# Expert chunks of eight slots in place of eleven, in a mixture-of-experts feed-forward kernel

## The chip, the cores and the metric

The kernel runs on one core of a Trainium2 chip. The metric is device time in microseconds (us). Engines: TensorE (PE; its weight loads are shown as PEld), VectorE (DVE), ScalarE (ACT), GpSimd (POOL) and SyncE (SP, which issues the DMAs).
## The reference, cut to what matters

A gate picks two of four experts for each of 64 samples of 64 tokens. Each expert is a two-layer network over all tokens of its samples; experts 1 and 2 leave out one third of a sample's tokens. A shared expert runs on all 4,096 tokens. A second stage, untouched here, does a gated feed-forward on every token and one of eight small experts on listed tokens.

```python
gate_scores = jax.nn.softmax(gate_logits, axis=-1)
topk_w, topk_i = jax.lax.top_k(gate_scores, K)          # K = 2, B = 64 samples
...
mask[1, L_head:L_head + L_wrist] = 0.0                  # one third of a sample
mask[2, :L_head] = 0.0
...
for e in range(E):                                      # E = 4
    h = jax.nn.gelu(context_c @ ew1[e] + eb1[e], approximate=True)   # 256 -> 1024
    y = h @ ew2[e] + eb2[e]                                          # 1024 -> 256
    out = out + w_be[:, e][:, None, None] * mask[e][None, :, None] * y
shared = jax.nn.gelu(context_c @ sw1 + sb1, approximate=True) @ sw2 + sb2
return out + shared
```

## The kernel before, in words

Weights and activations are held as pairs of float16 parts, high and low, and a product takes three matmuls (high x high, high x low, low x high). Work is cut into chunks of columns. A shared chunk has 256 columns (four samples). A sample is 66 columns wide with its borders, in three segments of SEG = 22; a *slot* is one segment of one sample for one expert. Experts 0 and 3 need three slots of a sample, 1 and 2 two (KEPT). An expert chunk has SLOTS slots of one expert, so RC = SLOTS x 22 = 242 columns, and each expert's last chunk is filled up with empty slots.

Per chunk, PE runs `hidden` (L1152): 8 blocks of the hidden layer x 3 x 2 = 48 matmuls into the four banks ps_hidden; then `output` (L1180) of the chunk before: 2 x 8 x 3 = 48 matmuls into ps_out. ACT applies gelu (L1022), DVE splits the result into high and low parts (L1325, L1327), ACT adds the bias of the output (L1113), and DVE adds each slot, times its gate weight, to the accumulator (`add_slots`, L1608). POOL copies the slots' columns together for the chunk two ahead (`stage_columns`, L1721). Slot addresses and the expert number of each chunk stand in the row tab, of SLOTS + 1 entries a chunk, which DVE makes from the gate's choice at run time. PE reads the expert number with `expert_of` (L1163) once for each half chunk, and the weights' addresses are computed from it:

```python
def w1(e, part, db, hb):
    return W[:, bass.ds(e * WE + (part * 2048 + db * 1024 + hb * P), P)]
```

Order on PE: shared chunks 0 to 13 (two more come late), the first hidden of the expert chunks, the output of shared chunk 13, then for r = 1, 2, ...: hidden(r), output(r-1). The program is written out chunk by chunk. Chunks up to NRMIN - 1 always run; the rest, up to NR, stand each in an If within the one before (`expert_loops`), with the count read once (L301) and compared at each (L283). NR is the largest count that any choice of the gate can need, NRMIN the smallest. After the last, a branch leads past the chunks not needed, to two late shared chunks, and then stage 2. Some small jobs are tied to a chunk number: index at 13, key matmuls (L1249) at 14, compare at 16 and 17, place (L1256, L1257) at 18, pack (L1263) at 20, listed at 21. Stage 2 uses L592, L604, L612, L625, L641.

Of the kernel before, what the change touches and what calls it, by code (L numbers as in the profile page):

```python
# [30 lines left out]
ALU = mybir.AluOpType  # L31
AX = mybir.AxisListType
# [12 lines left out]
SEG = NT - 2 * HEAD  # L45
BS = 3 * SEG
CB = CH // NT
SLOTS = 11
RC = SLOTS * SEG
KEPT = (3, 2, 2, 3)  # L50
KEPT0 = (0, 0, 1, 0)
NR = (2 * 3 * NB + E * (SLOTS - 1)) // SLOTS
NRMIN = -(-2 * 2 * NB // SLOTS)
NSLOT = NR * SLOTS
ROW = SLOTS + 1
NCNT = -(-3 * NB // SLOTS)
FAR = 16384
# [22 lines left out]
def program(nc, a):  # L80
    with ExitStack() as ctx:
# [80 lines left out]
        siota = xsw[0:NB, 2 * NSLOT:4 * NSLOT].bitcast(F32)  # L162
# [805 lines left out]
        def _(sp):  # L968
            for n, (dram, place, *_) in enumerate(opening):
                sp.dma_start(place, dram).then_inc(start_in[n], 16)  # L970
                if n == 1:
                    for dst, src in ((b1[:, :], a["b1"]), (b2[:, :], a["b2"])):
                        sp.dma_start(dst, src).then_inc(first_in, 16)
# [321 lines left out]
        def _(dve):  # L1295
            steps = [0]

            def link(i):

                steps[0] += 1  # L1300
                i.then_inc(dv, 1)
                dve.wait_ge(dv, steps[0])
# [180 lines left out]
            ce = yw[0:1, 0:4 * NR].rearrange("p (k r) -> p k r", k=4)  # L1483
# [5 lines left out]

            total, even = G[0:1, 27, 0:1], G[0:1, 27, 1:2]  # L1490
            link(nc.vector.tensor_tensor(total, G[0:1, 19, E - 1:E], G[0:1, 18, E - 1:E], ALU.add))
            link(nc.vector.tensor_scalar(ce[:, 0, 0:NR // 2], siota[0:1, 0:NR:2], total, None, ALU.is_lt))
            link(nc.vector.tensor_reduce(even, ce[:, 0, 0:NR // 2], AX.X, ALU.add))
            link(nc.vector.tensor_scalar(even, even, -2.0, 1.0, ALU.mult, ALU.add))
            link(nc.vector.tensor_tensor(even, even, total, ALU.add))
            link(nc.vector.tensor_scalar(total, total, -2.0, None, ALU.add))
# [287 lines left out]
```

## Time and profile before

| | us |
|---|---|
| median of 3 runs | 607.18 (607.03 to 607.24) |
| the profiled execution | 604.62 |
| its span, first to last instruction | 602.0 |
| PE busy | 567.1 (94%) |
| PE weight loads busy | 499.6 (83%) |
| DVE busy | 409.0 (68%) |
| ACT busy | 264.3 (44%) |
| POOL busy | 178.1 (30%) |
| mean granted TensorE clock | 0.979 |

Matmuls are pipelined, so a row's mean duration of one (267 ns) is a latency and not its share of the time; the distance from start to start is. "Issue" in the chain and in the waits is time in which an engine waited for nothing that the profile shows. The sequencer's own operations are not counted as busy.

### The profile page before, as it was taken

To read this page: it belongs to the slowest core of one execution; us is meant where nothing else is said; L and a number is where in the kernel's file an instruction comes from. 1 tells how busy PE (TensorE), PEld (TensorE's weight loads), DVE (VectorE), ACT (ScalarE), POOL (GpSimd) and SP (SyncE) were. 2 spreads that over 40 slices of the span, in tenths; PEclk is the share of its full clock that TensorE was granted. 3 is DMA by queue.
4 is the path that set the end of the run, shared out by engine and by line. 5 is a ranking of instruction groups with operands and counts; after the bars stand their busy time and mean duration, and the time that the engine had idled before them with its cause. 6 is when DMAs were issued, how large, how long until landed. Compare 5 with 4: busy or idle time off the path is not lost.

```text
span 602.0 us, 17044 instructions
## 1 busy us (share of the span) xinstructions
PE 567.1 (94%) x5093; PEld 499.6 (83%) x5094; DVE 409.0 (68%) x1092; ACT 264.3 (44%) x577; POOL 178.1 (30%) x529
## 2 busy tenths in 40 slices
PE   5999999999999999999999999999999979999770
PEld 4888888876899999999999999989999958667650
DVE  4969977757565868685677888756474735686560
ACT  6666667532444434344334343434343425464320
POOL 0350000000763444443424244443434002870000
PEclk9999999999999999999999999999999979999895
DMA  8812345001001232310000000000000001922130
GB/s 272 261 46 71 105 141 170 23 1 36 2 1 38 106 107 106 107 71 3 3 2 3 1 4 1 4 2 3 1 3 4 2 4 59 359 76 71 48 129 9
DMA packets 28482, 36.93 MB, mean 61 GB/s; under 512 B 4762, under 2 KB 24115, under 8 KB 28132
## 3 DMA queue, kind: packets, MB, share of 16 engines
q1 hardware_dynamic: 28292, 35.57, 18.0%
q8 instruction: 48, 0.79, 0.5%
q14 instruction: 46, 0.38, 0.2%
q0 software_dynamic: 96, 0.20, 0.1%
HBM read 27.30 MB, written 8.53 MB: 60 GB/s over the span
## 4 chain that ended last, share of the span: by engine, by line
PE 91%; DVE 3%; issue 1%; ACT 1%; DMA 1%; SPq 1%; POOL 0%; POOLq 0%; DVEq 0%
PE ps_out L1180 40%; PE ps_hidden L1152 39%; PE ps_hidden L592 3%; PE ps_hidden L641 1%; PE ps_out L612 1%; DMA W<-in_xT 1%; PE ps_turn L625 1%; PE ps_small L625 1%; PE ps_out L1223 1%; DVE X L782 1%; PE ps_out L604 1%; DVE hbuf L1327 0%; PE ps_hidden L625 0%; SPq L970 0%; DVE W L1311 0%
## 5 line engine op out<-in xcount | busy, mean ns | idle before, releaser
L1180 PE MATMUL ps_out<-hbuf,W 128*128 128x242 f16 (+2 forms) x2304 | 250.7, 269 | 0.7 <-DVE W L1311 0.6
L1180 PEld LDWEIGHTS ps_out<-hbuf,W 128*128 (+1 forms) x2304 | 223.8, 98 | 21.0 <-issue 1.3
L1721 POOL COPY xs<-X 128x88 f16 x352 | 128.4, 414 | 287.0 <-PE ps_hidden L1152 175.1
L1022 ACT ACTIVATE h<-ps_hidden,b 128x242 f32<-128x242 f32 (+1 forms) x384 | 155.8, 467 | 79.8 <-PE ps_hidden L1152 78.0
L1152 PE MATMUL ps_hidden<-xs,W 128*128 128x242 f16 x1536 | 164.2, 267 | 0.8 <-issue 0.8
L1152 PEld LDWEIGHTS ps_hidden<-xs,W 128*128 x1536 | 149.4, 98 | 10.8 <-issue 1.6
L1327 DVE TENSOR_TENSOR hbuf<-h,hbuf 128x484 f16<-128x484 f32 (+2 forms) x192 | 129.9, 676 | 7.4
L1608 DVE SCALAR_TENSOR_TENSOR acc<-ytmp,wrow,acc 128x44 f32 (+1 forms) x352 | 65.8, 259 | 92.4 <-ACT ytmp L1113 88.0
L1152 PE MATMUL ps_hidden<-X,W 128*128 128x256 f16 (+1 forms) x768 | 92.7, 283 | 10.3 <-DVE W L1311 6.1
L1325 DVE CAST hbuf<-h 128x484 f16<-128x484 f32 (+2 forms) x192 | 84.7, 441 | 22.4 <-ACT h L1022 21.2
L1152 PEld LDWEIGHTS ps_hidden<-X,W 128*128 128x128 f16 x768 | 76.6, 100 | 23.5 <-DVE W L1311 5.8
L1113 ACT ACTIVATE ytmp<-ps_out,b 128x242 f32<-128x242 f32 (+1 forms) x64 | 26.2, 460 | 133.4 <-PE ps_out L1180 133.4
L1031 ACT ACTIVATE acc<-ps_out,b 128x256 f32<-128x256 f32 x28 | 11.7, 470 | 41.0 <-PE ps_out L1180 41.0
L947 POOL COPY W<-acc 128x2 f32 x128 | 26.1, 338 | 2.8 <-issue 2.8
L1333 DVE SCALAR_TENSOR_TENSOR W<-stage,W 128x1024 f16<-128x1024 f32 x16 | 19.3, 1220 | 5.8 <-ACT W L1041 5.7
L1041 ACT ACTIVATE W<-stage 128x1024 f16<-128x1024 f32 x16 | 17.0, 1060 | 12.5 <-DMA stage<-in_ew 12.5
L592 PE MATMUL ps_hidden<-W,F 128*128 128x512 f16 x96 | 22.2, 379 | 0.0
L592 PEld LDWEIGHTS ps_hidden<-W,F 128*128 128x128 f16 x96 | 9.3, 100 | 10.0 <-DVE W L743 0.5
L953 POOL DMA_INDIRECT out_rows<-ytmp,sid x1 | 1.0, 1024 | 47.8 <-DVE ytmp L869 47.8
L940 POOL DMA_INDIRECT ytmp<-in_xR,gid x1 | 1.6, 1564 | 43.2 <-DVE f L1661 43.2
L612 PEld LDWEIGHTS ps_out<-onesm,W 128*128 128x128 f32 x64 | 8.8, 202 | 5.6 <-issue 4.7
L612 PE MATMUL ps_out<-onesm,W 128*128 128x1 f32 x64 | 8.1, 248 | 4.2 <-DVE stage L769 4.2
(291 smaller groups left out, 297.3 us busy)
## 6 DMA issues: line engine op xcount, KB each, us to landing
stage<-in_ew SPq DMA_DIRECT2D x16, 512.0 KB, 3.7
stage<-in_xR SPq DMA_DIRECT2D x8, 512.0 KB, 3.8
moved_rows<-stage SPq DMA_DIRECT2D x8, 512.0 KB, 2.6
X<-moved_rows SPq DMA_DIRECT2D x8, 512.0 KB, 9.2
out_rows<-X SPq DMA_DIRECT2D x16, 256.0 KB, 2.2
W<-in_xT SPq DMA_DIRECT2D x7, 512.0 KB, 9.2
W<-in_fw SPq DMA_DIRECT2D x1, 2304.0 KB, 12.5
W<-in_sw SPq DMA_DIRECT2D x4, 256.0 KB, 3.3
```

The source lines that it names most:

```text
L592: mm = pe.matmul(ps1[which][:, :], fw(wp, which, db), chl[:, k % CR, 2 * xp + db, :], start=(n == 0), stop=(n == 5))
L612: mm = pe.matmul(psy[1][:, k * MG + n:k * MG + n + 1], sq[:, k % 2, n * P:(n + 1) * P], onesm[:, 0:1], start=True, stop=True)
L947: i = nc.gpsimd.tensor_copy(cgT[:, :, at + j:at + j + 1], column(cols[j]))
L1022: i = nc.scalar.activation(h32[:, j, k * size:(k + 1) * size], ps1[j][:, k * size:(k + 1) * size], ACT.Gelu_apprx_tanh, bias=b1[:, bass.ds ...
L1113: i = nc.scalar.activation(ytmp[:, bass.ds(parity, 1), db, 0:RC].rearrange("p o c -> p (o c)"), psy2[:, bass.ds(parity, 1), db * RC:(db + ...
L1152: mm = pe.matmul(out, w1(e, wp, db, hb), rhs(xp, db), start=(n == 0), stop=(n == 5))
L1180: mm = pe.matmul(out, w2(e, wp, hb, db), h, start=(n == 0), stop=(n == 3 * HB - 1))
L1325: nc.vector.tensor_copy(hi, src).then_inc(h_hi, 1)
L1327: nc.vector.tensor_tensor(lo, src, hi, ALU.subtract).then_inc(h_ready, 1)
L1333: nc.vector.scalar_tensor_tensor(W[:, bass.ds(e * WE + (at + 2048), 1024)], stage[:, k % 2, :], WS, W[:, bass.ds(e * WE + at, 1024)], ALU. ...
L1608: i = nc.vector.scalar_tensor_tensor(at, y, wrow[:, bass.ds(r * SLOTS + j, 1)], at, ALU.mult, ALU.add)
L1721: i = nc.gpsimd.tensor_copy(xs[:, parity, :, j * SEG:(j + 1) * SEG], X[:, :, bass.ds(cols[j], SEG)])
```

## The change

Two edits. SLOTS goes from 11 to 8. With it RC goes from 242 to 176 columns, NR from 38 to 51, NRMIN from 24 to 32, so 19 chunks are conditional in place of 14, and the sizes that depend on them follow (the row of slots from 418 to 408, its table). The counting of even chunk numbers is widened by one where NR is odd.

```diff
-SLOTS = 11
+SLOTS = 8
 RC = SLOTS * SEG
...
-            link(nc.vector.tensor_scalar(ce[:, 0, 0:NR // 2], siota[0:1, 0:NR:2], total, None, ALU.is_lt))
-            link(nc.vector.tensor_reduce(even, ce[:, 0, 0:NR // 2], AX.X, ALU.add))
+            link(nc.vector.tensor_scalar(ce[:, 0, 0:(NR + 1) // 2], siota[0:1, 0:NR:2], total, None, ALU.is_lt))
+            link(nc.vector.tensor_reduce(even, ce[:, 0, 0:(NR + 1) // 2], AX.X, ALU.add))
```

The sizes that follow are set by:

```python
NR = (2 * 3 * NB + E * (SLOTS - 1)) // SLOTS
NRMIN = -(-2 * 2 * NB // SLOTS)
```

## Rows read from the trace of the kernel before

**Rows 1.** The page, chain that ended last, by engine and by line.
```profile
PE 91%; DVE 3%; issue 1%; ACT 1%; DMA 1%; SPq 1%; POOL 0%; POOLq 0%; DVEq 0%
```

**Rows 2.** Groups with shapes apart: count | busy us, mean ns | idle before.
```profile
L1152 PE MATMUL ps_hidden<-xs,W 128*128 128x242 f16 x1536 | 164.2, 267 | 0.8 <-issue 0.8
...
L1152 PE MATMUL ps_hidden<-X,W 128*128 128x256 f16 x480 | 59.3, 287 | 10.3 <-DVE W L1311 6.1 <-issue 4.2
...
L1152 PEld LDWEIGHTS ps_hidden<-xs,W 128*128 x1536 | 149.4, 98 | 10.8 <-issue 1.6
```

**Rows 3.** The chain in order of time, from 150 us: start, us, what.
```profile
157.08 5.24 PE ps_out L1180 x48
...
163.38 5.07 PE ps_hidden L1152 x48
...
173.69 4.96 PE ps_hidden L1152 x48
...
183.61 4.96 PE ps_hidden L1152 x48
...
521.02 2.59 PE ps_hidden L592 x12
```

**Rows 4.** Line 1152, 161.8 to 162.8 and 404.8 to 409.1 us: ns minimum/median/maximum, starts.
```profile
L1152 PEldq FUSED_REGOPS  x8: 46/46/46, 161.9 to 162.7; - x8
...
L1152 PEldq FUSED_REGOPS  x32: 46/46/51, 404.9 to 409.0; - x32
```

**Rows 5.** Line 1163, reads of the expert's number, in four windows.
```profile
L1163 PEldq TENSOR_LOAD <-tab x3: 299/302/308, 171.6 to 181.7; - x3
L1163 PEldq FUSED_REGOPS  x3: 151/151/156, 172.0 to 182.0; - x3
...
L1163 PEldq TENSOR_LOAD <-tab x15: 295/299/302, 231.4 to 300.8; - x15
...
L1163 PEldq TENSOR_LOAD <-tab x3: 297/300/301, 373.3 to 383.2; - x3
...
L1163 PEldq TENSOR_LOAD <-tab x5: 295/297/302, 409.1 to 429.2; - x5
```

**Rows 6.** The chain in order of time, jobs tied to chunks and the late chunks.
```profile
312.57 0.90 PE ps_turn L1249 x8
...
353.15 0.13 PE ps_small L1256 x2
353.28 0.22 PE ps_small L1257 x2
...
373.36 0.48 PE ps_small L1263 x20
...
374.05 5.15 PE ps_hidden L1152 x48
...
404.40 0.56 issue
404.97 5.16 PE ps_hidden L1152 x48
```

**Rows 7.** Busy time by engine, one conditional chunk.
```profile
425.20:435.20 10.00, 10.00 (x98) 9.09 (x98) 6.02 (x19) 4.08 (x10) 3.66 (x11) 1.00 0.01 2
```

**Rows 8.** The jump: its branch (L283), the chain, the stretch's granted clock.
```profile
L283 PEldq COMPARE_BRANCH  x1: 3815/3815/3815, 484.2 to 484.2; - x1
...
485.35 4.15 issue
489.50 7.78 PE ps_hidden L1152 x48
...
489.50:497.30 7.80, 7.80 (x50) 5.93 (x51) 2.51 (x5) 2.52 (x6) 0.00 (x0) 0.70 0.00 1
```

**Rows 9.** Line 1263, twenty loads and matmuls of 4 columns.
```profile
L1263 PEld LDWEIGHTS ps_small<-vals,stage x20: 95/96/98, 373.1 to 373.6; 128*128 128x128 f16 x20
```

**Rows 10.** Busy time by engine (PE first) and granted clock in stage 2.
```profile
580.00:585.00 5.00, 3.61 (x17) 2.84 (x15) 4.86 (x15) 0.00 (x0) 0.00 (x0) 1.00 0.33 108
```

## The prediction, made before the changed kernel was run

> **What bounds the kernel now.** I began with the page's chain of the work that ended last. TensorE holds 91% of it, nearly all in two lines: L1180, the output matmuls, and L1152, the hidden matmuls [rows 1]. Next I read PE's groups with shapes kept apart: the expert chunks have 1,536 hidden matmuls, 48 a chunk, so there are 32 of them, each with 48 output matmuls as well; PE sat idle 0.8 us in all before the hidden ones, and before those of the shared chunks 10.3 us, of which 6.1 are in the opening and 4.2 are unexplained "issue" [rows 2].
>
> The chain in order of time gives what one half chunk of 48 matmuls costs: 4.96 us at 242 columns, 5.24 us at 256; and 12 matmuls of 512 columns take 2.59 us [rows 3]. Per matmul that is 103.3, 109.2 and 215.8 ns. The three lie on one line, columns / 2.4 GHz + 2.5 ns. Read alone, this says that the array is the bound and that fewer columns are time saved.
>
> So I looked at what feeds the array. Each weight slice of an expert chunk has an address held in a register (e*WE + constant), so PE's instruction sequencer runs a register operation for each new slice. It has its own rows, marked PEldq: 32 in each half chunk, for 48 weight loads and 48 matmuls [rows 4]. In hidden(24) they stretch from 404.9 to 409.0 us, 31 steps in 4.1 us. Is that pace set by the sequencer, or does the array hold it back? The stretch ahead of the first expert chunk tells: 8 of them start from 161.9 to 162.7 us, while the first matmul of that chunk starts at 163.4 us [rows 3, 4]. Seven steps in 0.8 to 0.9 us is about 0.12 us a step, with none of the chunk in the array. It is the sequencer's own pace. Each half also starts with reading the expert's number: a load of 0.30 us, a register operation of 0.15 some 0.4 us behind its start, and about 0.64 us in all from the load to the first address [rows 5].
>
> The marker of one half to the next is that load. Over two halves: 373.3 to 383.2, so 9.9 us a chunk; in conditional chunks 409.1 to 429.2 over four halves, 10.05 us a chunk [rows 5]. The array's own need is 2 x 4.96 = 9.92. **The two are equal**: at 242 columns the array just covers the sequencer. Early on the sequencer is ahead (load at 171.6 and 181.7, matmuls of those halves at 173.7 and 183.6 [rows 3, 5]); from about 374 us it is not (load at 373.3, matmuls at 374.05), the chain has "issue" in it, and the eight conditional chunks take 404.97 to 485.35 us, 10.05 us each [rows 5, 6]. That is the sequencer's pace, not the array's.
>
> The other engines are far from it: in 10.0 us of a conditional chunk DVE works 6.02, ACT 4.08, POOL 3.66 us [rows 7].
>
> **The change part by part.** *How many chunks.* The number is set by the inputs. Working the gate of the reference in high precision (its smallest margin between the second and third expert is 0.0056, so float noise moves none), experts 0 to 3 get 10, 51, 6 and 61 samples; times KEPT (3, 2, 2, 3) that is 30, 102, 12 and 183 slots, 327 in all. In chunks of eleven: 3 + 10 + 2 + 17 = 32, as the trace has it. In chunks of eight: 4 + 13 + 2 + 23 = 42. Unconditional ones go from 24 to 32, taken conditional ones from 8 to 10.
>
> *What it saves on the array.* Columns go from 32 x 242 = 7,744 to 42 x 176 = 7,392. By the line above a 176-column matmul takes 75.8 ns, a half 3.64 us, a chunk 7.28 us: 84 x 3.64 = 305.8 against 64 x 4.96 = 317.4 us, a gain of 11.6 us, if the array is the bound.
>
> *What it costs on the sequencer.* Nothing in the instruction stream of a chunk depends on its columns: still 96 loads, 96 matmuls, 64 addresses, two expert numbers. I take 9.9 us for an unconditional chunk and 10.05 for a taken conditional one [rows 5]. As 9.9 is more than 7.28, the array no longer hides the sequencer, and the longer of the two is the chunk.
>
> *Sum*, from the start of hidden(1), 173.69 us, to the end of the last output before the jump, 485.35 us: 311.7 us before [rows 3, 6]. After: 31 x 9.9 = 306.9; 10 x 10.05 = 100.5; the matmuls of key 0.90, place 0.13 + 0.22 and pack 374.05 - 373.36 = 0.69 stay [rows 6]; first conditional entry 0.56 and one stray gap of 0.15 doubled to 0.3, as they will be no better hidden. In all 410.2. From it come off, at the start, 4.96 - 3.64 = 1.3 for hidden(0), whose addresses are prepared early, and about 1.1 of lead that the sequencer has there (1.9 - 0.8 us, the distances from load to matmul at 181.7 and 373.3) and spends once. Net 410.2 - 311.7 - 2.4 = **+96.1 us**.
>
> *The rest.* The jump out of the conditional chunks stays one jump: its branch takes 3.8 us, the engine is idle 4.15, and the half behind runs 7.78 us instead of 5.24 at a clock of 0.70 [rows 8]; kept, since that wait is long over what a shorter chunk alters. DVE's table building has a grid of 408 columns for 418 and a count of 51 for 38 rows: nothing, as it works behind shared chunks, where PE's idle time is that of the opening and of the jump [rows 2]. The corrected (NR + 1) // 2 counts the even chunks for an odd NR: 26 elements, nothing. ACT, DVE and POOL have a third more chunks, but of 8 slots: even at unchanged 6.02 us a chunk DVE stays below 9.9, and POOL's copies wait on PE, not PE on them. The jobs tied to a chunk number (index at 13, compare at 16 and 17, listed at 21) keep the same 9.9 us between them. Stage 2 is untouched.
>
> *Weight loads.* A load shows 98 ns [rows 2], above 75.8, and could be a floor of its own. But 20 loads and 20 matmuls of 4 columns start within 0.5 us, 26 ns a pair [rows 9]: loads overlap. The Trainium skill, page "TensorE: Matmul & The Clock Gate", section "LDWEIGHTS (loading the stationary operand)", gives columns / 1.2 GHz, 107 ns for 128, which would put a load-bound chunk at 96 x 107 = 10.2 us, and speaks against the change; the 26 ns pair does not bear it out as a pace. The same page, in "Wait — 56ns, not 53.3ns?", says that a sequencer that decodes matmuls in software needs some 62 ns for each. By that alone 96 x 62 = 6.0 us would fit under the array's 7.28, and the change would gain; it counts no address operations, and the pace here, 32 steps for 48 pairs, is about 83 ns a pair plus the expert number.
>
> **The rivals.** *A, the array stays the bound.* Should the sequencer's pace be due to back-pressure from the array after all, it would speed up with the matmuls: 607.2 - 11.6 = 595.6, faster. For it: the two paces are suspiciously equal, and fifteen loads from 231.4 to 300.8 us come every 4.96 us, the array's own period [rows 5]. Against: the pace with the array empty of this work, and the "issue" in the late chunks. It decides the case if the address step falls below about 0.08 us ((3.64 - 0.64 - 0.3 for the rest) / 32). 6%.
>
> *B, loads serialize at 98 ns and the sequencer is cheaper than I think.* A chunk would be 96 x 98 = 9.4 us: 42 x 9.4 - 317.4 = +77, so 684. Against: the 26 ns pair. 3%.
>
> *C, the clock falls.* The array has 7.3 us of columns in each 9.9. At the lower level, 1.2 GHz, a matmul takes 147 ns, a chunk 14.1 us, the whole 882; with a quarter of the chunks there, 703 + 10.5 x 4.2 = 747. Against: 580 to 585 us has PE busy 3.61 of 5 us at clock 1.00, and the gaps in a chunk are under 1 us, where the fall at 485 us followed 4.15 us of nothing [rows 8, 10]. 4%.
>
> *D, stalls now hidden come out.* A program half as long again without any lead over the array may show every late instruction fetch. If each chunk lost 0.4 us, 720. 6%.
>
> **How the numbers follow.** The forecast: 607.2 + 96.1 = 703.3 us, chance 81%. The profiled execution (span 602.0, 604.62 us with what lies around it) would come to 698 and 701; its 2.6 us below the median I leave as it is. If a chunk is 9.8 us, 699; if 10.1, 711; with the start's 2.4 us or the one-offs in doubt, 697 to 713 is the range. It leaves out A, B, C and D, 19%. Faster by over 0.2% (about what a measurement of this kernel can tell from no change) is A, 6%; within it 1%; slower 93%.
>
> **What would show it.** PE's L1152 rows at 176 columns with 2,016 matmuls on expert chunks; the expert-number load every 4.9 to 5.0 us throughout, with the matmuls 0.8 us behind it; PE idle put down to "issue" in each half, and a chain with far more issue in it. A chunk period near 7.3 us refutes the sequencer, and 14 us points to the clock. Most likely to make me wrong: a sequencer that does better than 9.9 us once nothing holds it up.

## The result and the profile after

The changed kernel takes **703.34 us** (702.32 to 704.35), the kernel before 607.21 (607.03 to 607.63): a ratio of 1.158 (1.156 to 1.160). The forecast was 703.3 us, in a range of 697 to 713. The profiled execution is the longest of the four: 704.35 us with a span of 702.5.

The chain's shares on the page, which answer to [rows 1]: PE has lost 13 points, issue has won 8 and DVE 4 (what the DVE share is worth is told under cut11).

```profile
PE 78%; issue 9%; DVE 7%; ACT 1%; DMA 1%; SPq 1%; DVEq 0%; ACTq 0%; POOL 0%; POOLq 0%
```

Groups with shapes apart, as [rows 2]: 2,016 hidden matmuls are 42 chunks of 48. PE is busy 183.0 us on them against 164.2, and idle 21.8 us before them where it was 0.8.

```profile
L1152 PE MATMUL ps_hidden<-xs,W 128*128 128x176 f16 x2016 | 183.0, 241 | 21.8 <-issue 21.7
L1180 PE MATMUL ps_out<-hbuf,W 128*128 128x176 f16 x1968 | 178.3, 242 | 28.8 <-issue 19.2 <-DVE hbuf L1327 9.5
```

One chunk in the chain in order of time, to be held against [rows 3], and the reads of the expert's number, as [rows 5]:

```profile
403.03 4.42 PE ps_hidden L1152 x48
407.45 0.59 issue
408.04 4.36 PE ps_out L1180 x48
412.39 0.52 issue
412.91 4.39 PE ps_hidden L1152 x48
...
L1163 PEldq TENSOR_LOAD <-tab x3: 298/301/305, 402.3 to 412.1; - x3
...
L1152 PEldq FUSED_REGOPS  x31: 46/46/46, 403.1 to 407.0; - x31
```

The chunk is 9.88 us, two halves of 4.4 us with matmuls and two gaps of 0.5 to 0.6 us in which the expert's number is read. A half of 48 matmuls takes not the array's 3.64 us but 4.4, so the array waits within the half too, for address after address: 31 address operations start from 403.1 to 407.0 us, 0.13 us apart. "Busy" hides that, as each matmul's row is 239 ns long and the next begins within it. The read is at 402.3 and the matmul behind it at 403.03: the sequencer has no lead, in this chunk as in all behind the first two, except those with a job on PE (point 2 of the section on why).

### The profile page after: what moved, and what is told of

Its sections match the earlier page's. It is cut to its first block, busy times and chain, and to the rows that moved or that the text cites. A ratio compares the mean times of both kernels' runs of the same rounds, so it can differ in the third digit from the quotient of the medians.

```text
span 702.5 us, 20003 instructions
## 1 busy us (share of the span) xinstructions
PE 616.5 (88%) x6053; PEld 493.6 (70%) x6054; DVE 419.8 (60%) x1156; ACT 282.5 (40%) x677; POOL 160.5 (23%) x513
## 4 chain that ended last, share of the span: by engine, by line
PE 78%; issue 9%; DVE 7%; ACT 1%; DMA 1%; SPq 1%; DVEq 0%; ACTq 0%; POOL 0%; POOLq 0%
PE ps_out L1180 37%; PE ps_hidden L1152 31%; PE ps_hidden L592 3%; DVE hbuf L1327 2%; DVE acc L1608 1%; DVE hbuf L1325 1%; PE ps_hidden L641 1%; PE ps_out L612 1%; DMA W<-in_xT 1%; PE ps_turn L625 1%; PE ps_hidden L625 1%; PE ps_small L625 1%; PE ps_out L1223 1%; ACT ytmp L1113 0%; DVE X L782 0%
## 5 line engine op out<-in xcount | busy, mean ns | idle before, releaser
L1180 PE MATMUL ps_out<-hbuf,W 128*128 128x176 f16 (+2 forms) x2784 | 269.9, 250 | 29.7 <-issue 19.2
L1180 PEld LDWEIGHTS ps_out<-hbuf,W 128*128 (+1 forms) x2784 | 216.0, 97 | 82.3 <-issue 40.6
L1022 ACT ACTIVATE h<-ps_hidden,b 128x176 f32<-128x176 f32 (+1 forms) x464 | 170.1, 426 | 109.3 <-PE ps_hidden L1152 109.2
L1721 POOL COPY xs<-X 128x88 f16 x336 | 111.0, 378 | 399.8 <-PE ps_hidden L1152 287.2
L1152 PE MATMUL ps_hidden<-xs,W 128*128 128x176 f16 x2016 | 183.0, 241 | 21.8 <-issue 21.7
L1608 DVE SCALAR_TENSOR_TENSOR acc<-ytmp,wrow,acc 128x44 f32 (+1 forms) x336 | 63.5, 259 | 159.9 <-ACT ytmp L1113 157.6
L1327 DVE TENSOR_TENSOR hbuf<-h,hbuf 128x352 f16<-128x352 f32 (+2 forms) x232 | 134.4, 579 | 8.8
L1325 DVE CAST hbuf<-h 128x352 f16<-128x352 f32 (+2 forms) x232 | 89.4, 385 | 37.8 <-ACT h L1022 31.8
L1113 ACT ACTIVATE ytmp<-ps_out,b 128x176 f32<-128x176 f32 (+1 forms) x84 | 29.8, 404 | 182.2 <-PE ps_out L1180 182.2
L750 DVE SCALAR_TENSOR_TENSOR W<-ps_hidden,stage,W 128x512 f32<-128x512 f32 x8 | 6.0, 750 | 8.6 <-ACT W L492 5.1
## 6 DMA issues: line engine op xcount, KB each, us to landing
W<-in_fw SPq DMA_DIRECT2D x1, 2304.0 KB, 11.9
```

The source lines that it names most:

```text
L1022: i = nc.scalar.activation(h32[:, j, k * size:(k + 1) * size], ps1[j][:, k * size:(k + 1) * size], ACT.Gelu_apprx_tanh, bias=b1[:, bass.ds ...
L1113: i = nc.scalar.activation(ytmp[:, bass.ds(parity, 1), db, 0:RC].rearrange("p o c -> p (o c)"), psy2[:, bass.ds(parity, 1), db * RC:(db + ...
L1152: mm = pe.matmul(out, w1(e, wp, db, hb), rhs(xp, db), start=(n == 0), stop=(n == 5))
L1180: mm = pe.matmul(out, w2(e, wp, hb, db), h, start=(n == 0), stop=(n == 3 * HB - 1))
L1325: nc.vector.tensor_copy(hi, src).then_inc(h_hi, 1)
L1327: nc.vector.tensor_tensor(lo, src, hi, ALU.subtract).then_inc(h_ready, 1)
```

## The experiments

All times are medians. The kernel before ran beside each group of runs and took 607.8 us in the first (603.6 to 609.8), 607.8 in the second (605.9 to 611.1) and 607.9 in the third (605.1 to 610.2), so what rests on under 3 us is read from the traces. Chunk periods are the distances between the starts of PE's hidden halves.

**Fewer columns, the same number of chunks.** This takes the change apart: 32 chunks, but matmuls of 176 columns.

```diff
-  lambda xp, db: xs[:, parity, 2 * xp + db, 0:RC], RC)
+  lambda xp, db: xs[:, parity, 2 * xp + db, 0:CUT], RC, CUT)      # CUT = 8 * SEG; the same in output
```

> The kernel before, 32 chunks of eleven slots, but each expert matmul works on 176 of the chunk's 242 columns; the last three slots of each chunk are left out of the products. Everything else, the instruction count of every engine too, stays. Theory S (PE's sequencer sets a chunk, about 9.9 us whatever the columns): the time stays near before, 604 to 612 us, a chunk of 9.9 us with PE idle in it. Rival A (the array is the bound and feeds back on the sequencer): each half takes 3.64 in place of 4.96 us, 64 x 1.32 = 84 us less, 523 us. Rival D (a fixed cost per chunk comes from other engines) agrees with S here; static8 tells them apart.

Measured: 599.5 us, ratio 0.989 (0.982 to 0.996). The chunk is 9.86 us, with the array working on 27% fewer columns than before. Rival A's 523 us is out. The time is 4.5 us below my band. By hidden(31) the trace is 5.6 us ahead of before: the first two chunks gain 2.6 us from the lead, some twenty more come at 9.86 instead of 9.92 us, and the jobs on PE tied to chunks no longer add their time. **The 9.9 us do not come from the columns.** Whether they belong to PE's instruction stream or to a loop of waits between the engines (rival D of the expectation) this run can't tell; the next one does.

Three lines of its chain are worth a look, as they mislead:

```profile
413.30 0.68 DVE hbuf L1330
413.98 0.54 issue
414.52 4.34 PE ps_out L1183 x48
```

They say that the output half waits for DVE's split of the hidden layer, and the page of the changed kernel charges DVE with 7% in the same way. But this split belongs to the chunk whose hidden half has just run; the output half is that of the chunk before, split long ago. The semaphore that it checks was counted up last by DVE, no more. The run without address operations bears that out.

**No address operations.** The weights of expert 1 at fixed addresses, the rest of the changed kernel as it is.

```diff
-            return W[:, bass.ds(e * WE + (part * 2048 + db * 1024 + hb * P), P)]
+            e = e if isinstance(e, int) else 1
+            at = e * WE + (part * 2048 + db * 1024 + hb * P)
+            return W[:, at:at + P]        # the same in w2
```

> The changed kernel with the weights of expert 1 at fixed addresses in every expert chunk, so that PE has no address operation; the choice of the expert is left out of the products, the number is still read twice a chunk. All other engines do what they do in the changed kernel. Theory S: with 32 address operations gone from each half the array becomes the bound, a chunk of 7.3 us, 607.2 - 11.6 = 596 us, up to 605 if plain loads and matmuls have a price of their own on the sequencer. Rival D (the 9.9 us are the loop of semaphores between PE, ACT, DVE and POOL): the chunk stays near 9.9 us and the time within 10 us of 703.

Measured: 602.7 us (598.2 to 604.1), ratio 0.991 (0.988 to 0.995). The chain has nothing but matmuls:

```profile
381.30 3.64 PE ps_out L1184 x48
384.94 3.64 PE ps_hidden L1156 x48
388.58 3.64 PE ps_out L1184 x48
```

A chunk is 7.28 us, to the digit what the line through three column counts gave. Two reads a chunk are still there, so reads, 96 loads and 96 matmuls together fit in 7.28 us. All four other engines did the full work of 42 chunks, so no loop of semaphores holds the chunk at 9.9: **the 9.9 us belong to PE's instruction stream.** The total is 7 us above my 596. The larger part is what a shorter chunk uncovers, DVE's jobs of chunks 16 and 17: PE waits once for 3.18 us, and the half behind takes 5.45 us in place of 3.64, at a granted clock of 0.69:

```profile
297.18 3.80 PE L1156 MATMUL ps_hidden<-xs,W 128*128 128x176 f16 x48
304.16 5.45 PE L1184 MATMUL ps_out<-hbuf,W 128*128 128x176 f16 x48 [3.18 <-DVE hbuf L1331]
309.44 0.32 PE L1260 MATMUL ps_small<-f,tri 128*128 128x8 f32 x2
...
304.16:309.61 5.45, 5.45 (x50) 5.45 (x51) 4.60 (x16) 0.70 (x2) 0.18 (x1) 0.69 0.00 0
```

That chunk took 12.66 us, 5.4 more than its neighbours, and three others 8.1 to 8.2. At the jump the idle time and the half behind come to 13.15 us, 1.2 more than before.

**The same with eleven slots.** The same edit in the kernel before.

> The kernel before with the weights of expert 1 at fixed addresses in every expert chunk, so without address operations on PE; the choice of the expert is left out of the products. Theory S: at 242 columns the array needs as long as the sequencer, so only the late chunks gain, 11 chunks x 0.1 us and the 0.9 us of issue gaps, 605 us. A rival by which address operations cost the array time one for one (2048 x 0.046 us) gives 513 us; one by which they cost nothing at all gives 607.

Measured: 601.3 us (598.4 to 603.8), ratio 0.987 (0.984 to 0.990). But for the three with jobs on PE, every chunk comes at 9.92 us, the late ones too: there the array is the bound, with nothing between the halves. This is 4 us less than expected. By the trace 2.0 us of that are at the jump: 3.02 us of idle and 6.85 for the half behind, against 4.15 and 7.78. The rest I can't place; the runs spread over 5.4 us.

**Addresses in one half only.**

```diff
-            return W[:, bass.ds(e * WE + (part * 2048 + db * 1024 + hb * P), P)]
+            e = e if isinstance(e, int) else 1            # in w1 alone; w2 keeps its operations
...
```

> The changed kernel with fixed weight addresses in the hidden halves alone (expert 1's first layer in every expert chunk; the choice of the expert is left out there); the output halves keep their 32 address operations. Theory S: the hidden half falls to the array's 3.64 us and the output half stays at 4.95 to 5.0, a chunk of 8.6 to 8.7 us, 703.3 - 42 x 1.3 = 649 us, between 645 and 660. Rival D: near 703.

Measured: 626.6 us (one run), a chunk of 8.0 us. That is 0.6 us a chunk less than I expected and about the length of a read. The chain has one gap a chunk instead of two, before the hidden half:

```profile
402.29 3.73 PE ps_out L1182 x48
406.02 0.46 issue
406.48 3.81 PE ps_hidden L1154 x48
410.29 3.83 PE ps_out L1182 x48
...
L1165 PEldq TENSOR_LOAD <-tab x1: 302/302/302, 408.8 to 408.8; - x1
```

The sequencer is done early with the hidden half and reads the next number, and a few addresses, while the array is still on it: the read is at 408.8, 1.5 us before the array ends the half. So the two halves share a budget, and I was wrong to take the larger for each half by itself. They don't share all of it: the sum would be 9.87 - 32 x 0.124 = 5.9 us on the sequencer, under the array's 7.28, and the chunk takes 8.0. A lead that ends at 1.5 us would explain that: from this read to the first matmul of the next hidden half the sequencer has two reads and 32 addresses to do, 2 x 0.70 + 32 x 0.124 = 5.4 us, and the array has 1.5 + 3.64 = 5.1 us of work. No run varied the lead.

**A quarter fewer.** 24 address operations a half.

```diff
+            if part == 1 and hb % 2 == 1 and not isinstance(e, int):
+                return W[:, WE + (part * 2048 + db * 1024 + hb * P):WE + (part * 2048 + db * 1024 + hb * P) + P]        # the same in w2
             return W[:, bass.ds(e * WE + (part * 2048 + db * 1024 + hb * P), P)]
```

> The changed kernel with a quarter of the weight slices (the low parts at odd hidden blocks) at fixed addresses, those of expert 1, in every expert chunk, so that a half has 24 address operations in place of 32; for these slices the choice of the expert is left out. If each address operation costs the sequencer its 0.124 us from start to start, a chunk falls from 9.87 to 9.87 - 16 x 0.124 = 7.9 us: 703 - 42 x 2 - 3 (the reads lie elsewhere against the copies) = 616 to 622 us. If it costs the 0.046 us that its row shows as its duration, the chunk falls to 9.1 us, 672 us. If the loads and matmuls set the pace (0.03 us each instruction, addresses included), to 9.87 - 16 x 0.031 = 9.4 us, 682 us.

Measured: 617.2 us (one run), a chunk of 7.82 us. (9.87 - 7.82) / 16 = **0.128 us an address operation**. The row gives each 0.046 us, so its duration is a third of its price. The loads and matmuls between add nothing: 16 steps went, with all 192 other instructions in place, and 16 whole steps of time went with them.

**One read a chunk.** A complete kernel: the output half uses the number that the hidden half before it had read.

```diff
-                hidden(r + R0, expert_of(r), lambda ...
+                held.append(expert_of(r))
+                hidden(r + R0, held[-1], lambda ...
...
-                output(r + (R0 - 1), expert_of(r - 1), 1 - parity, RC)
+                output(r + (R0 - 1), held[-2], 1 - parity, RC)
```

> The changed kernel, complete, but the output half takes the expert number that the hidden half of the same chunk had read one step before, so PE reads it once a chunk. Theory S: 0.64 us a chunk from load to first address go, 41 x 0.64 = 26 us, 677 us. Rival A or D: the read is hidden beside other work and the time stays at 703.

Measured: 670.2 us, ratio 1.105 (1.097 to 1.113). Unconditional chunks take 9.17 us, conditional ones 9.33. A read costs 0.70 us, a little over my 0.64: 41 x 0.70 = 29. Most of the other 4 us went in chunks 3 to 10, where no read was long any more (297 to 312 ns), for the reason that the next run tests.

**The slow chunks 3 to 10.** In the changed kernel these eight come every 10.25 to 10.57 us, the ones after them every 9.87. In them one read of two is long, as the maximum shows; the kernel before, same stretch of its program, has none:

```profile
L1163 PEldq TENSOR_LOAD <-tab x12: 296/506/849, 190.6 to 247.2; - x12
...
194.45 0.34 SPq L443 DMA_DIRECT2D moved_rows<-stage  x1
```

```profile
L1163 PEldq TENSOR_LOAD <-tab x17: 295/300/316, 186.6 to 266.0; - x17
```

The read at 195.6 us falls into the copy issued at 194.45, which from 195.2 to 196.6 us keeps the DMA engines full. Before, the copy was issued at 197.8 and the reads stood at 196.5 and 201.5. In the experiment the copy is small:

```diff
-                sp.dma_start(a["xc"][j], stage[:, s, :]).then_inc(xc_out[s], 16)
+                sp.dma_start(a["xc"][j][:, 0:128], stage[:, s, 0:128]).then_inc(xc_out[s], 16)
...
```

So that stage 2 has whole rows, a second edit has it read them from the input, without the addition:

```diff
-                             a["xc"][k].rearrange("p (n d) -> p n d", d=D)).then_inc(x_rows_in[k], 16)
+                             a["xR"][k * FC:(k + 1) * FC, :].rearrange("(n p) d -> p n d", p=P)) \
+                    .then_inc(x_rows_in[k], 16)
```

> The changed kernel in which the copies of rows to memory, issued in chunks 3 to 10, carry 128 of 1024 columns; DVE's addition before them (1.2 us) stays, and stage 2 reads the rows without that addition, which is left out of the result. In the changed kernel the read of the expert number takes 0.70 to 0.87 us in place of 0.30 in exactly these eight chunks, while such a copy is in flight. Theory: the read waits for the DMA engines or for memory that they hold; the read goes back to 0.30 us, chunks 3 to 10 from 10.3 to 9.9 us, 3.4 us less, 700 us. Rival: DVE's addition is what PE waits for, as the profile's releaser says; the reads stay at 0.7 us and the time at 703.3.

Measured: 700.6 us (700.4 to 701.7), against 703.3. The reads:

```profile
L1164 PEldq TENSOR_LOAD <-tab x13: 297/301/312, 190.4 to 249.8; - x13
```

The eight chunks take 9.86 to 10.02 us. DVE's addition is still there (1.22 us), so it was not what PE waited for, whatever the chain names. The read of a register from on-chip memory waits for a large copy that reads the same memory.

Is it enough that the DMA engines are busy? The next run, s10, answers that, as its reads fall into the other copy, the one *into* on-chip memory:

```profile
198.71 0.37 SPq L436 DMA_DIRECT2D stage<-in_xR  x1
...
201.20:201.50 0.30, 0.30 (x6) 0.30 (x4) 0.00 (x0) 0.00 (x0) 0.00 (x0) 1.00 1.07 382
...
L1163 PEldq TENSOR_LOAD <-tab x13: 297/299/314, 191.3 to 250.8; - x13
```

At 201.2 us the DMA engines are as full (1.07) as in the changed kernel at 195.6 us (1.05), and the read takes 0.30 us; six reads of s10 and six of cut11 fall into such a copy, and none is long. So it is the copy out of on-chip memory that holds the read. At what place it does is not shown.

**Ten slots.** A check on the count of chunks (s10).

```diff
-SLOTS = 8
+SLOTS = 10
```

> The changed kernel with ten slots in place of eight: 3 + 11 + 2 + 19 = 35 chunks of 220 columns, 7,700 columns in all, 44 fewer than before. Theory S: time goes with the number of chunks, three more than before at 9.9 us, less the 2 us of lead at the start and up to 3 us more of stalls: 635 to 641 us. Rival A: the array's 35 x 96 x 94.2 ns = 316.4 us against 317.4, 606 us.

Measured: 631.8 us, ratio 1.039 (1.035 to 1.043), 24 us over before with 44 columns fewer. The chunk is 9.87 us; 35 of them. Some 3 us below my band: I left the jobs on PE in the sum, as in the second point of the next section, and no read was long.

**Eleven slots with one read.** The same edit as in reuse8, on the kernel before.

> The kernel before, complete, but the output half takes the expert number that the hidden half had read one step before. Theory S: the sequencer then needs 9.3 us a chunk against the array's 9.92, so the late chunks fall from 10.05 to 9.92 us and the gaps at 374 to 404 us close: 607.2 - 1.6 = 605.6 us, 0.2 to 0.3% less. Rival A: 607.2.

Measured: **603.1 us** (601.0 to 607.3), ratio 0.992 (0.989 to 0.995): a gain of under 1%, but clear of none, and the fastest complete kernel. Late chunks are at the array's pace, and two things more happen at the jump. Against [rows 8]:

```profile
478.01 4.96 PE ps_out L1183 x48
482.97 2.85 issue
485.82 5.57 PE ps_hidden L1152 x48
491.39 5.18 PE ps_out L1183 x48
...
485.80:491.40 5.60, 5.58 (x50) 4.88 (x51) 1.73 (x6) 2.52 (x6) 0.00 (x0) 1.00 0.02 6
```

The last output half ends at 482.97 instead of 485.35. The sequencer reaches the branch 2.0 us before that end instead of 1.1, and the branch itself took 3.31 us instead of 3.82, so the array idles 2.85 us instead of 4.15; and the granted clock stays at its upper level (1.00 in the window), where it had fallen, so the next half takes 5.57 us and not 7.78. Sum: 2.4 + 1.3 + 2.2 = 5.9 us by the trace; the times show 4.7. The clock is seen at its upper level behind the jump in this one profile; in those of the eleven other kernels the idle time is 3.0 to 6.2 us, and the clock fell in each.

**Ten slots with one read.** Is eleven the best size once the read is cheaper?

> Ten slots, complete, with the expert number read once a chunk: 35 chunks of max(array 9.04, sequencer 9.17) us = 321 us against 32 x 9.92 = 317.4, so 3 to 4 us slower than eleven slots with one read, and 3 to 5 us faster than the kernel before less what its late chunks lose: 604 to 607 us.

Measured: 611.0 us, ratio 1.005 (1.003 to 1.007), slower than both. The chunks are as expected, 9.04 where the array and 9.2 where the sequencer is the bound. What I left out: the chunks with jobs take 9.7 to 10.4 us, as the array, which has to do the jobs on PE, is the bound again, and PE waits 0.3 us for DVE in one of them; the late chunks take 9.3 each; and the jump again idles 4.1 us, with 7.18 us for the half behind it. Against the trace of reuse11 the last output half ends 7.1 us later, and the jump costs 2.8 us more.

## Why the prediction was right, and where only in the sum

1. *The number of chunks and the sequencer as the bound*: right. 42 chunks; 9.85 to 9.89 us in most unconditional ones against my 9.9, 10.0 in the conditional ones against 10.05. cut11 has the pace with fewer columns, static8 without address operations, fewer8 in proportion.
2. *The one-off jobs on PE*: wrong in kind. I kept key, place, pack and a stray gap, 2.2 us, as additions. In the changed kernel the twenty chunks from 11 to 30, with all three jobs among them, take 0.4 us more than twenty times 9.87: the chunk with key takes 10.13 us and the next one 9.70, together 0.1 us over two others:

```profile
313.25 0.93 PE ps_turn L1249 x8
314.18 3.98 PE ps_hidden L1152 x48
```

   The sequencer runs on during those eight matmuls, and the half behind them takes 3.98 us instead of 4.4. An array with 2.6 us of slack in each chunk swallows them.
3. *Chunks 3 to 10*: a term that I didn't have. Eight reads of 0.70 to 0.87 us in place of 0.30, and 10.37 us a chunk: 8 x (10.37 - 9.9) = 3.7 us. I had gone through the queues for what is moved past what, and not asked which transfers a read would now meet.
4. *The start*: right. Hidden(1) begins 8.98 us after hidden(0), 10.31 before: 1.3 us, as said; the next one begins 8.54 us later and so 1.4 us short of 9.9, against 1.1.
5. The stretch from hidden(1) to the jump came to 582.60 - 172.92 = 409.7 us against 410.2 - 1.1 = 409.1 forecast. The small difference is a sum of misses of both signs: 3.7 us from point 3 and 0.4 from the entry into the conditional chunks (that chunk 10.89 us, forecast 10.46) on the one side; on the other 1.8 from point 2 with its stray gap, 0.6 from a pace of 9.87 instead of 9.9 in chunks 11 to 30, 0.7 from the last chunk, which takes 9.39 us as no gap stands behind it, and 0.3 each from the start and the other conditional chunks. **Point 3 and the rest cancel**: that the total matches to 0.1 us is luck, that it lies within some 4 us is not.
6. *The jump* kept its price as a sum: 4.88 us of idle and 6.99 for the half, 11.9 together, as before. The parts differ, 4.15 and 7.78 before; that they cancel is luck again, as in cut11 they come to 13.2.
7. The two profiled executions differ by 99.7 us, the medians by 96.1. In stage 2 of the one of after, the lower clock lasted longer:

```profile
668.25 2.58 PE ps_hidden L625 x12
...
662.00:680.00 18.00, 17.18 (x93) 13.22 (x94) 7.78 (x26) 3.89 (x11) 0.00 (x0) 0.72 0.34 117
```

   The same twelve matmuls took 1.33 us in the profile of before. As reuse11's profile, with eleven slots, has 2.58 there as well, it needs no change of slots to come about. Behind the jump and its half chunk, the profile of after is 3.3 us longer than that of before.

Of the rivals, A fell with cut11. B, loads one behind another at 98 ns, would make a chunk 9.4 us; static8 has 7.28 us with all 96 loads in place, 76 ns each. The rate of columns / 1.2 GHz for a load (107 ns for 128) from "LDWEIGHTS (loading the stationary operand)" on the Trainium skill's page "TensorE: Matmul & The Clock Gate" does not hold as a pace here. C: the granted clock stayed at 1.00 through the expert chunks (its 882 us should be 703 + 42 x 4.2 = 879). D, instruction fetches that come out, was not seen: 9.85 to 9.89 us leave no room for 0.4 us a chunk. Point 3 is a stall of another kind, in eight chunks, at under a quarter of D's price. What was argued and not shown is how the 0.128 us divide between the operation and the hand-over of a load that depends on it, and what bounds the sequencer's lead (half8).

## What to carry to other kernels

Count the instructions that each tile costs the sequencer, addresses from registers above all, and hold their distance from start to start against the tile's array time: where the two meet, smaller tiles buy nothing and each further tile costs the full sequencer time. Look for the pace in a stretch where the array cannot be what holds it back. And when a chain blames an engine by a semaphore, check in the code which item that wait is for.

## What the runs showed of the hardware

- On PE, in these kernels, an operation that computes the address of a weight load costs 0.124 to 0.128 us from start to start, though its row shows 0.046 us. Loads and matmuls that need no new address add nothing that could be seen beside 7.28 us for 96 of each.
- A read of a number from on-chip memory into a PE register, with the arithmetic behind it, costs 0.70 us of the stream; the read itself takes 0.30 us, and up to 0.87 us while a 512 KB copy out of the same memory is in flight. A copy into it, with the DMA engines as full, leaves it at 0.30 us.
- A branch past code not run took PE's sequencer 3.3 to 5.0 us in the twelve traces. How much of it the array feels depends also on the work queued before it: 2.85 us of idle and no fall of the clock in reuse11, 3.0 to 6.2 us and a fall in the eleven others (4.15 us and a half chunk of 7.78 us in the kernel before).
